# Cross attention: norms of 8 of 16 key heads as a quadratic form on VectorE, fewer split tiles, one more shift on GpSimd

## What is computed

```python
q = (hidden_states @ Wq).reshape(B, Sq, H, D)            # B=16, Sq=56, H=16, D=128
k = (encoder_hidden_states @ Wk).reshape(B, Skv, H, D)   # Skv=1500, context of 128 channels
v = (encoder_hidden_states @ Wv).reshape(B, Skv, H, D)
q = rmsnorm(q, gq)
k = rmsnorm(k, gk)
attn = softmax(einsum('bqhd,bkhd->bhqk', q, k) * scale)
out = einsum('bhqk,bkhd->bqhd', attn, v).reshape(B, Sq, H * D) @ Wo
```

## Time and profile before

| | |
|---|---|
| median of three runs | 1323.13 us (1322.19 to 1323.25) |
| span of the profiled execution | 1321.1 us |
| TensorE busy | 1290.7 us (98%) |
| VectorE busy | 1155.3 us (87%) |
| GpSimd busy | 1089.0 us (82%) |
| ScalarE busy | 1074.3 us (81%) |
| mean granted TensorE clock | 0.996 of full |

### The profile page before, as it was taken

How to read it: one execution, slowest core, us unless ns; L and a number is a source line. 1 busy time by engine, 2 the same in 40 slices (tenths; PEclk the granted TensorE clock), 3 DMA queues, 4 the chain that set the end, 5 groups by cost and what they waited for, 6 DMA issues and landing times.

```text
span 1321.1 us, 21768 instructions
## 1 busy us (share of the span) xinstructions
PE 1290.7 (98%) x6516; PEld 1059.3 (80%) x6516; DVE 1155.3 (87%) x1777; ACT 1074.3 (81%) x3171; POOL 1089.0 (82%) x922
## 2 busy tenths in 40 slices
PE   8989999999999999999999999999999999999998
PEld 5767677788888888888888888888888888878787
DVE  5866689999999999999999999999999999997755
ACT  2667788899999999999999999999899999973442
POOL 5644452989999999999999999999999999999840
PEclk9989999999999999999999999999999999999999
DMA  7140230101010101010101010101010101030300
GB/s 254 46 160 1 80 136 13 36 13 36 13 36 12 36 12 36 13 36 13 36 13 36 13 36 13 35 13 36 13 36 10 38 9 40 1 112 1 115 24 29
DMA packets 27845, 54.12 MB, mean 41 GB/s; under 512 B 2816, under 2 KB 22400, under 8 KB 25936
## 3 DMA queue, kind: packets, MB, share of 16 engines
q1 hardware_dynamic: 26736, 52.38, 11.8%
q10 hardware_dynamic: 992, 0.36, 0.1%
HBM read 44.60 MB, written 8.13 MB: 40 GB/s over the span
## 4 chain that ended last, share of the span: by engine, by line
PE 83%; ACT 5%; DVE 5%; POOL 4%; issue 3%; ACTq 0%; POOLq 0%; DVEq 0%
PE xa_k_ps L1419 12%; PE xa_k_ps L1420 11%; PE xa_k_ps L1421 11%; PE xa_s_ps L1420 5%; PE xa_s_ps L1421 5%; PE xa_s_ps L1419 5%; PE xa_o_ps L1419 5%; PE xa_o_ps L1421 4%; PE xa_o_ps L1420 4%; PE om_ps L1516 3%; PE xa_o_ps L1510 3%; PE xq_ps L634 2%; POOL xa_den L1170 1%; POOL probs_r L1184 1%; DVE xa_ss L1349 1%
## 5 line engine op out<-in xcount | busy, mean ns | idle before, releaser
L1349 DVE TENSOR_REDUCE xa_ss<-xa_sq 125x6 f32<-125x768 f32 x360 | 339.5, 943 | 3.7 <-ACT xa_sq L1267 2.2
L1184 POOL TENSOR_TENSOR probs_r<-probs,xa_p_hi 125x896 fp32r<-125x896 f32 (+1 forms) x160 | 330.4, 2065 | 5.3
L1419 PE MATMUL xa_k_ps<-wk_parts,xa_ctxT_hi 128*125 128x512 f32 x768 | 324.0, 422 | 6.2 <-ACT xa_sq L1267 5.9
L1420 PE MATMUL xa_k_ps<-wk_parts,xa_ctxT_hi 128*125 128x512 f32 x768 | 302.8, 394 | 0.0
L1421 PE MATMUL xa_k_ps<-wk_parts,ctxT_lo 128*125 128x512 f32 x768 | 302.4, 394 | 0.0
L1336 DVE TENSOR_TENSOR xa_scores<-xa_s_ps,xa_rk 125x448 f32<-125x448 f32 x384 | 237.8, 619 | 50.8 <-PE xa_s_ps L1421 48.4
L1170 POOL TENSOR_TENSOR xa_den<-probs,xa_den 125x896 f32<-125x896 f32 x128 | 272.8, 2131 | 3.7 <-ACT probs L1248 3.7
L1226 ACT ACTIVATE xa_sq<-xa_k_ps 125x512 f32<-125x512 f32 x360 | 213.8, 594 | 26.0 <-DVE xa_ss L1349 16.6
L1248 ACT ACTIVATE probs<-xa_scores 125x896 f32<-125x896 f32 x192 | 182.8, 952 | 57.0 <-POOL xa_scores L1159 35.1
L1266 ACT ACTIVATE xa_k_ps<-xa_k_ps 125x128 f32<-125x128 f32 x720 | 193.9, 270 | 21.6 <-PE xa_k_ps L1421 21.3
L1357 DVE TENSOR_TENSOR xa_max_ps<-xa_scores,xa_max_ps 125x448 f32<-125x448 f32 x320 | 198.1, 619 | 0.6
(11 more groups left out here) (187 smaller groups left out, 2479.1 us busy)
## 6 DMA issues: line engine op xcount, KB each, us to landing
xa_ctx_nat<-in_ctx SPq DMA_DIRECT2D x16, 750.0 KB
ctxT_in<-in_ctxT SPq DMA_DIRECT2D x84, 125.0 KB, 2.1
qo<-in_xo_w SPq DMA_DIRECT2D x1, 2048.0 KB, 16.7
qo<-in_xq_w SPq DMA_DIRECT2D x1, 2048.0 KB, 15.3
vo_scratch<-qo SPq DMA_DIRECT2D x2, 1024.0 KB, 4.0
w_parts_scratch<-ws_hi SPq DMA_DIRECT2D x2, 1024.0 KB, 4.1
w_parts_scratch<-ws_lo SPq DMA_DIRECT2D x2, 1024.0 KB, 5.3
vo<-vo_scratch SPq DMA_DIRECT2D x1, 2048.0 KB, 8.8
```

The costliest lines, as they stand in the source:

```text
L1184: pool.tensor_tensor(probs_r[0:KP, slots, :], probs[0:KP, slots, :], p_hi[:, y // 2 % (NPR // 2), first:2, :].bitcast(F32), ALU.subtract). ...
L1349: dve.tensor_reduce(ss[:, i // 2, UH * (i % 2):UH * (i % 2) + vector_heads(of)], squares(of, i).rearrange("p (g d) -> p g d", d=XD), AX.X, ...
L1419: pe.matmul(out, l_hi, r_hi, start=first, stop=False)
L1420: pe.matmul(out, l_hi, r_lo, start=False, stop=False)
```

## The change

- Four of the eight heads of a step (those of `project_k(ph, j, 0)`) get their norm without keys. With G = W W' of the head (128 by 128), the sum of squares is c'Gc. TensorE forms G once, from `xq_wkT`, at the end of the query part (`gram`); its rounded and low parts take the place of those heads' columns in `wk_hi` and `wk_lo`. A step then multiplies the rounded context by G's two parts (two products in place of three).
- VectorE multiplies the result with a tile `ctx_m` and sums over the 128 channels: one `tensor_tensor_reduce` for each head, which the program issues as two instructions, the product and a readout of its accumulator. To make up for the dropped product, `ctx_m` holds the context minus half its rounded value.
- `ctx_m` is loaded in three parts of four tiles an element (`load_m`), rounded and halved by ScalarE (`round_m`, 512 wide) and subtracted by GpSimd (`take_half`).
- ScalarE squares and sums all four heads of the second bank with accumulators. L1226, L1267 and VectorE's L1349 are gone.
- Tile pairs 1 and 2 of a half become plain float32 products (`PAIR_SPLITS` from five split pairs to three), so their rounded exponentials and low parts go; in the last element one tile of each of the two pairs.
- The shift at t = 8 goes from VectorE to GpSimd (`VS`, `GS` from 5, 1 to 4, 2).
- `project_k(ph, j, 0)` waits for `squared` (ScalarE, two steps back), `project_k(ph, j, 1)` for `formed` (VectorE, one step back).

The core of the diff:

```diff
...
+            def gram(i):
+
+                pe.wait_ge(qn_ready, V - 3 if i == 0 else V)
+                for g in range(QH):
+                    head = wkT[:, GRAM_HEADS[i] + g, :]
+                    mm = pe.matmul(ps[:, GRAM_BANKS[i], g * C:(g + 1) * C], head, head, start=True, stop=True)
+                mm.then_inc(gram_mm, 1)
...
-VECTOR_SHIFTS = {2: 0, 3: 2, 5: 4, 7: 6, 8: 8}
-VS, GS = 5, 1
+VECTOR_SHIFTS = {2: 0, 3: 2, 5: 4, 7: 6}
+VS, GS = 4, 2
...
-PAIR_SPLITS = (0, 2, 2, 2, 2, 2)
+FIRST_SPLIT = 3
+PAIR_SPLITS = (0, 0, 0, 2, 2, 2)
...
-LAST_SPLITS = (0, 1, 1, 1, 1, 1)
+LAST_SPLITS = (0, 0, 0, 1, 1, 1)
...
+            def load_m(ph, part):
+
+                wait(sp, formed, ph.at(STEPS, 2 * MT * (part + 1)) if ph.b >= 0 else 0)
+                src = a.ctx[ph.b + 1].rearrange("(p t) c -> p t c", t=KT)
+                sp.dma_start(m_tiles(part), src[:, MT * part:MT * (part + 1), :]).then_inc(m_loaded[part], 16)
...
+                if ph.b == -1:
+                    for part in range(KT // MT):
+                        load_m(Phase(0), part)
+                        if part < 2:
+                            mlp.store_parts(sp, part)
...
+            def take_half(ph, part):
+
+                pool.wait_ge(m_hi_ready, m_count(ph, part))
+                pool.tensor_tensor(m_tiles(part), m_tiles(part), m_hi[:, :, :].bitcast(F32), ALU.subtract
+                                   ).then_inc(m_ready, 1)
...
+            def round_m(ph, part):
+
+                act.wait_ge(m_loaded[part], 16 * (ph.b + 2))
+                wait(act, m_ready, m_count(ph, part) - 1)
+                act.activation(m_hi[:, :, :], m_tiles(part), ACT.Copy, scale=0.5).then_inc(m_hi_ready, 1)
...
-                    if ph.within(-1, 14):
-                        wait(act, k_done, ph.at(2 * STEPS, 2 * STEPS + 2 * j + 1))
-                        wait(act, summed, ph.at(STEPS, STEPS + j - 1))
-                        act.activation(squares(ph, j)[:, 0:4 * XD], k_ps[0:KP, (2 * j) % 3, :], ACT.Square
-                                       ).then_inc(squared, 1)
...
+                        for g in range(UH - GH):
+                            head = UH * (j % 2) + GH + g
                             cols = k_ps[0:KP, (2 * j + 1) % 3, g * XD:(g + 1) * XD]
...
+                            last = act.activation(cols, cols, ACT.Square, scale=MEAN ** 0.5,
+                                                  accum_out=ss[:, j // 2, head:head + 1])
+                        last.then_inc(squared, 1)
...
+                    if ph.within(-1, 14):
+                        if j % (2 * MT) == 0:
+                            dve.wait_ge(m_ready, m_count(ph, j // (2 * MT)))
+                        dve.wait_ge(k_done, ph.at(2 * STEPS, 2 * STEPS + 2 * j + 1))
+                        for g in range(GH):
+                            cols = k_ps[0:KP, (2 * j) % 3, g * C:(g + 1) * C]
+                            head = UH * (j % 2) + g
+                            form = dve.tensor_tensor_reduce(cols, cols, ctx_m[:, j // 2, :], 2 * MEAN, 0.0, ALU.mult, ALU.add,
+                                                            ss[:, j // 2, head:head + 1])
+                        form.then_inc(formed, 1)
...
-                    if (ph.within(-1, 14) and j >= 1) or (ph.within(0, 15) and j == 0):
-                        i = (j - 1) % STEPS
-                        of = ph if j >= 1 else ph.shift(-1)
-                        dve.wait_ge(squared, ph.at(2 * STEPS, 2 * STEPS + 2 * j))
-                        dve.tensor_reduce(ss[:, i // 2, UH * (i % 2):UH * (i % 2) + vector_heads(of)],
-                                          squares(of, i).rearrange("p (g d) -> p g d", d=XD), AX.X, ALU.add
-                                          ).then_inc(summed, 1)
...
+                if c == 0:
+                    pe.matmul(out, ctxT_hi[:, i, t, :], wk_hi[:, cols], start=True, stop=False)
+                    return pe.matmul(out, ctxT_hi[:, i, t, :], wk_lo[:, cols], start=False, stop=True)
...
-                        wait(pe, squared, ph.at(2 * STEPS, 2 * STEPS + 2 * j - 2))
+                        wait(pe, squared, ph.at(STEPS, STEPS + j - 1))
...
-                        wait(pe, squared, ph.at(2 * STEPS, 2 * STEPS + 2 * j - 1))
+                        wait(pe, formed, ph.at(STEPS, STEPS + j))
...
```

## The result

The changed kernel takes **1316.32 us** (median; 1316.16 to 1316.45) where the kernel before took 1323.18 beside it: a ratio of 0.9948, 95% interval 0.9934 to 0.9962. It is faster by 0.5%; the forecast of 1339 us was slower by 1.2%. The profiled execution has a span of 1314.4 us (before: 1321.1).

A forecast was written before the change was run, and what follows sets the result against it. VectorE was to become the bound at 67.1 us a phase against 66.0; with 0.2 for leaks, 1.3 us times 14 phases gave +18, less 2 at the ends, plus 2.0 from span to median: 1339 us, range 1290 to 1400.

The forecast's parts named there:

- d: On VectorE, time from the start of one product-and-readout pair to the next, taken as 0.265 us; 96 pairs a phase.
- the level point: The d at which VectorE's need equals the time before the change: 0.253 us, 0.012 below the value taken.
- the first rival: VectorE's accumulator readout almost free, d between 0.20 and about 0.25; 1293 us at 0.23; chance 0.25.
- The formula: VectorE's need a phase: 61.9 - 20.6 - 2.0 + 2.4 + 96 d = 41.7 + 96 d us.
- the added shift: On GpSimd's queue, ahead of a sum; ScalarE's exponential waits for it, claimed no later than the sixth pair's shift now.
- allowed for leaks: 0.2 us a phase added to VectorE's need, for TensorE's plain-product steps not fully covered by its lead.
- Phase -1: Stage before phase 0: TensorE 5.5 us shorter, but phase 0 waits for stored split weights; 2 us taken as gain.
- the G products: Eight TensorE products forming G, once, beside the query part's end: costed at nothing, at most 1 us if unhidden.
- TensorE's 61.6 us: TensorE's time a phase: 66.0 - 5.5 for dropped products + 1.1 for plain tiles.
- GpSimd's 62.2: GpSimd's us a phase: 62.6 with four low parts less, two shifts and three `take_half` more.
- the 0.12 us of uncovered wait: On VectorE, scores to maximum 0.65 us apart instead of 0.53, in 20 steps: +2.4 us a phase.
- the plain tiles' price: On TensorE, eight tiles a phase from split to plain, 0.14 us each: +1.1 us a phase.

The follow-up runs named there:

- e7: Changed kernel with ScalarE's rounding of the second natural-context part two steps later and GpSimd's shift ahead of the low part in its step: 1299.22 us.
- e11: e7 with, in phase -1, the first weight store ahead of the product-row load, whose rounding on ScalarE comes four steps later: 1297.78 us.

## Why the prediction was wrong

**The step that failed is the size of d.** "I take d = 0.265" was 0.20 for the product and 0.065 for the readout, as if the readout paid the fixed part of an instruction. The product was nearly right (0.21); the readout adds 0.04 where the next product starts with it, and nothing where the scores do. 96 x (0.265 - 0.239) = 2.5 us a phase, 35 us in 14 phases, and with it the sign: the level point was 0.253. What happened is the mechanism of the first rival. The formula itself held: 41.7 + 96 x 0.239 = 64.6 us, and e7, where VectorE waits for nothing, needs 64.5. Part of that closeness is luck: its 61.9 is what VectorE is busy in a 66 us window, and over the 14 whole phases of the kernel before VectorE is busy 62.4 us a phase (873.91 us from 244.45 to 1174.49), with which the formula gives 65.2. Of the two sections of the Trainium skill's "VectorE: DVE Perf Modes" that the prediction set against each other, the trace sides with "Two Vector instructions with no wait between them": the readout is a record of its own and starts 0.21 us after a product that lasts 0.29. What "The DRAIN you can't avoid" would make of it, 0.437 us, is not seen; that section itself refers to the other one for an instruction that is not held.

**Waits that were given no price.** I cleared ScalarE and GpSimd by their busy times. I wrote of the added shift that it "comes no later than the sixth pair's shift does now". For its own pair, the fifth, that held: the exponential of that pair has no long wait. Wait A is at the sixth pair's shift. It is an old wait, stood in the earlier trace rows (21.2 us) and got no price. From ScalarE's rounding, for which GpSimd's low part waits, to that pair's exponential it takes 3.4 us in both kernels in the half below. What changed is ScalarE, whose squares in between take less time, so that it arrives sooner and waits longer. The same place of a half, before and after:

```profile
676.49 0.41 ACT L1214 ACTIVATE xa_ctxT_hi<-ctxT_in 128x250 fp32r<-128x250 f32 x1
...
679.87 0.96 ACT L1248 ACTIVATE probs<-xa_scores 125x896 f32<-125x896 f32 x1 [1.09 <-POOL xa_scores L1159]
```

```profile
676.53 0.40 ACT L1269 ACTIVATE xa_ctxT_hi<-ctxT_in 128x250 fp32r<-128x250 f32 x1
...
679.88 0.95 ACT L1306 ACTIVATE probs<-xa_scores 125x896 f32<-125x896 f32 x1 [1.82 <-issue]
```

So the wait grew to 33.0 us. Wait B is new and I did not see it: the rounding's place in the steps was left while its buffer came free later. 0.2 us was allowed for leaks; 65.61 is 1.0 above VectorE's 64.6.

**The phase of before.** I took the 66.0 us of the window in the earlier trace rows as the length of a phase. It is 66.43, as the starts show. That is 0.43 x 14 = 6 us too little credit.

**Phase -1.** Two us were to come back, 5.1 went. TensorE's five products did not shorten the step. These are TensorE's first instructions of three steps in a row, 1.42 us apart on average, where the six products of the kernel before took 1.39 (164.47 to 165.86 us in its timeline):

```profile
164.91 0.50 PE L1496 MATMUL xa_k_ps<-wk_parts,xa_ctxT_hi 128*125 128x512 f32 x1
...
166.40 0.47 PE L1496 MATMUL xa_k_ps<-wk_parts,xa_ctxT_hi 128*125 128x512 f32 x1
...
167.75 0.50 PE L1496 MATMUL xa_k_ps<-wk_parts,xa_ctxT_hi 128*125 128x512 f32 x1
```

In each such step TensorE now waits for the release of a bank, by ScalarE's squares and by VectorE's products:

```profile
164.90 0.18 PEld L1496 LDWEIGHTS xa_k_ps<-wk_parts,xa_ctxT_hi 128*125 128x125 f32 x1 [0.34 <-ACT xa_k_ps L1323]
...
165.48 0.18 PEld L1485 LDWEIGHTS xa_k_ps<-wk_parts,xa_ctxT_hi 128*125 128x125 f32 x1 [0.28 <-DVE xa_ss L1393]
```

I let phase 0 start when the split weights are stored. VectorE does check that, but what holds up its first product of phase 0 is TensorE's key product. TensorE is late because it needs a low part of the context from GpSimd every four steps, and on GpSimd's queue these stand behind the split weights. GpSimd stood 5.67 us for the first store (2.32 before), which shares the transfers with the new load (us to landing 6.2 instead of 4.1, and 4.5 in e11), and TensorE stopped twice. The second of its rows names ScalarE's rounding, which ends at the same time; the low part that this step needs starts at 186.14, right behind the last split weight.

```profile
193.39 0.30 DVE L1393 CUSTOM_DVE_ANT_0 xa_k_ps<-xa_k_ps,xa_ctx_m 125x128 f32<-125x128 f32 x1 [0.39 <-PE xa_k_ps L1497]
```

```profile
174.86 0.61 POOL L1722 CAST ws_hi<-ws_raw 128x512 fp32r<-128x512 f32 x1 [5.67 <-DMA w_parts_scratch<-ws_hi]
```

```profile
179.52 0.47 PE L1496 MATMUL xa_k_ps<-wk_parts,xa_ctxT_hi 128*125 128x512 f32 x1 [1.06 <-POOL ctxT_lo L1155]
...
186.96 0.47 PE L1496 MATMUL xa_k_ps<-wk_parts,xa_ctxT_hi 128*125 128x512 f32 x1 [1.72 <-ACT xa_ctxT_hi L1269]
```

1.9 us of the 5.1 are shown by e11. 1.2 were lost in the query part already, where I costed the G products at nothing, at most 1 us. They stand in TensorE's stream in two groups, whose next instruction starts 0.90 and 0.95 us later. The first group, and then GpSimd's low part ahead of the weights, before and after:

```profile
145.28 1.05 PE L644 MATMUL xq_ps<-xq_wkT 128*128 128x128 f32 x8
...
146.18 0.60 PE L625 MATMUL xq_ps<-ident,xq_qn 128*128 128x128 f32 x4
```

```profile
156.39 0.73 POOL L1113 TENSOR_TENSOR ctxT_lo<-ctxT_in,xa_ctxT_hi 128x250 fp32r<-128x250 f32 x1
```

```profile
157.62 0.72 POOL L1155 TENSOR_TENSOR ctxT_lo<-ctxT_in,xa_ctxT_hi 128x250 fp32r<-128x250 f32 x1
```

The other 2 us no run shows; the two stops of TensorE can hold part of them.

**The sum again:** 1339 - 35 (d) + 14 (1.0 a phase of ScalarE's waits) - 3 (0.2 of allowed leak) - 6 (phase of before) + 7 (phase -1) - 3 (phase 15, which I had at nothing) + 2 (phase 0 and the end) = 1315, measured 1316.3. The errors partly cancel: with the right d alone I would have said 1304.

**What held.** TensorE's 61.6 us to within 1.1 (62.7 a phase by busy time, 63.08 / 66 x 65.61), GpSimd's 62.2 (61.1), ScalarE below 60 (53.4), the 0.12 us of uncovered wait, the plain tiles' price, and VectorE as the fullest engine above 97%. The last line on what would make it wrong named ScalarE's chain by way of GpSimd's shift, which is wait A; I named it and gave it no price.

## What to carry to other kernels

Price a string of small instructions by their distance from start to start; where the level point lies 0.012 us from the value taken, within what no row shows, let neither side have much more than the other. When one engine's work shrinks, go through every engine's waits in program order, the idle engines' too: a freed engine arrives early at an old wait, and a step left in its place may now come before its buffer is free. Two such waits, one behind the other, gave back little one at a time (0.2 and 3.9 us alone, 17.1 together).

## What the runs showed of the hardware

VectorE's product with an accumulated sum, 128 wide from PSUM, repeats every 0.25 us although its two records last 0.33 and 0.14; the readout costs 0.04 between two products. ScalarE's readout costs 0.09 in the kernel before. And ScalarE, by the page of the profile the least busy engine of the changed kernel (74%), cost it 17 us by where it waited.
